# One place later: the large products beside scores and context sums in an attention kernel

## The reference, cut to what matters

```python
h_q = (x @ w_q.T).reshape(b, lq, H, DH)          # x normalised
h_k = (key_value_states @ w_k.T).reshape(b, lk, H, DH)
h_v = (key_value_states @ w_v.T).reshape(b, lk, H, DH)
score = jnp.einsum('bqhd,bkhd->bhqk', h_q, h_k) + position_bias[None]
score = jax.nn.softmax(jnp.where(m, score, -jnp.inf), axis=-1)
attn = jnp.einsum('bhqk,bkhd->bqhd', score, h_v).reshape(b, lq, H * DH)
out = attn @ w_out.T                             # then the residual, and the feed-forward layer
```

## Time and profile before

| | us |
|---|---|
| median of three runs | 820.9 (820.55 to 822.34) |
| the profiled execution | 820.63, its span 818.8 |
| TensorE busy | 799.6 (98% of the span) |
| VectorE busy | 636.1 (78%) |
| ScalarE busy | 361.6 (44%) |
| GpSimd busy | 305.9 (37%) |
| TensorE's granted clock, mean | 0.999 |
| attention rounds 3 to 13 | about 409 to 731 |

### The profile page before, as it was taken

How to read it: one execution, slowest core, us unless ns; L and a number is a source line. 1 busy time by engine, 2 the same in 40 slices (tenths; PEclk the granted TensorE clock), 3 DMA queues, 4 the chain that set the end, 5 groups by cost and what they waited for, 6 DMA issues and landing times.

```text
span 818.8 us, 12698 instructions
## 1 busy us (share of the span) xinstructions
PE 799.6 (98%) x4090; PEld 674.9 (82%) x4090; DVE 636.1 (78%) x1066; ACT 361.6 (44%) x949; POOL 305.9 (37%) x279
## 2 busy tenths in 40 slices
PE   9999999999999999999999999999999999999998
PEld 8888888888888888887888887888788888888886
DVE  6877868977873796988878877877877787777775
ACT  6633432432331344544444444444444444447683
POOL 3103111021020034726455545635545544545136
PEclk9999999999999999999999999999999999999999
DMA  8365575584474749337556565565655646653002
GB/s 305 131 219 175 191 245 168 156 289 133 155 228 158 242 163 313 127 101 229 158 177 211 159 205 187 156 198 178 209 167 172 227 149 207 187 186 142 1 1 104
DMA packets 103217, 145.54 MB, mean 178 GB/s; under 512 B 9944, under 2 KB 74584, under 8 KB 97648
## 3 DMA queue, kind: packets, MB, share of 16 engines
q1 hardware_dynamic: 102720, 144.33, 54.5%
q10 hardware_dynamic: 432, 0.39, 0.1%
HBM read 93.31 MB, written 51.38 MB: 177 GB/s over the span
## 4 chain that ended last, share of the span: by engine, by line
PE 95%; issue 2%; DVE 1%; ACT 1%; DMA 0%; POOL 0%; SPq 0%; DVEq 0%
PE out L1438 11%; PE out L1440 11%; PE out L1439 11%; PE proj L1438 10%; PE proj L1440 10%; PE proj L1439 10%; PE o L1558 7%; PE s L1532 7%; PE s L1439 4%; PE s L1440 4%; PE s L1438 4%; PE proj L1634 1%; PE proj L1635 1%; PE t L1586 1%; PE t L1542 1%
## 5 line engine op out<-in xcount | busy, mean ns | idle before, releaser
L1005 ACT ACTIVATE probs<-probs,neg_max 128x128 f32<-128x128 f32 x256 | 99.7, 391 | 120.6 <-DVE neg_max L1270 120.6
L835 POOL TENSOR_TENSOR w_stage<-w_stage 128x256 f32<-128x256 f32 x30 | 26.7, 892 | 278.2 <-DMA w_stage<-in_wk 242.1
L1438 PE MATMUL out<-wo_hi,o_hi 128*128 128x512 f32 x224 | 91.6, 409 | 13.2 <-issue 13.2
L847 POOL TENSOR_TENSOR w_lo<-w_stage,w_hi 128x512 fp32r<-128x512 f32 (+1 forms) x52 | 64.3, 1245 | 101.3 <-ACT w_hi L951 101.3
L1440 PE MATMUL out<-wo_lo,o_hi 128*128 128x512 f32 x224 | 88.0, 393 | 0.0
L1439 PE MATMUL out<-wo_hi,o_lo 128*128 128x512 f32 x224 | 87.4, 390 | 0.0
L1438 PE MATMUL proj<-x_hi,w_hi 128*128 128x512 f32 x210 | 85.3, 406 | 0.9 <-POOL w_lo L847 0.6
L1315 DVE TENSOR_TENSOR acc<-out,acc 128x512 f32<-128x512 f32 x100 | 67.8, 678 | 20.5 <-PE out L1440 20.5
L1440 PE MATMUL proj<-x_lo,w_hi 128*128 128x512 f32 x210 | 82.4, 392 | 0.0
L1439 PE MATMUL proj<-x_hi,w_lo 128*128 128x512 f32 x210 | 82.0, 391 | 0.0
L859 POOL TENSOR_TENSOR bias_mask<-bias_raw,mask_neg 128x512 f32<-128x512 f32 x64 | 76.2, 1191 | 13.0 <-DVE probs L1267 11.8
(11 more groups left out here) (360 smaller groups left out, 2078.4 us busy)
## 6 DMA issues: line engine op xcount, KB each, us to landing
k_spill<-ring SPq DMA_DIRECT2D x64, 256.0 KB, 3.5
v_spill<-ring SPq DMA_DIRECT2D x64, 256.0 KB, 2.6
p_turned<-probs SPq DMA_DIRECT2D x208, 64.0 KB, 1.8
probs_t<-p_turned SPq DMA_DIRECT2D x52, 256.0 KB, 4.0
big_stage<-in_wv SPq DMA_DIRECT2D x8, 1024.0 KB, 7.5
w_stage<-in_wq SPq DMA_DIRECT2D x32, 256.0 KB, 3.1
k_first<-k_spill SPq DMA_DIRECT2D x8, 1024.0 KB, 6.0
v_first<-v_spill SPq DMA_DIRECT2D x8, 1024.0 KB, 5.0
```

The lines of the kernel that those rows point to most:

```text
L847: pool.tensor_tensor(lo, staged(m, part), hi.bitcast(F32), ALU.subtract).then_inc(g_wlo, 1)
L1005: last = act.activation(probs[:, j % 2, b, :], probs[:, j % 2, b, :], ACT.Exp, bias=neg_max[:, col:col + 1], accum_out=row_sum[:, col:col ...
L1438: pe.matmul(to[:], left_hi, right_hi, start=first and n == 0, stop=False, skip_group_check=True)
```

## The change

The number of steps is the same, each on the same engine; only the order of the list is different, in the rounds 0 to 13. In rounds 2 to 13, for TensorE:

| place | large products before | after |
|---|---|---|
| A | OUT0, P1, OUT1, OUT2 | P4 of the group before, OUT0, P1, OUT1 |
| B | OUT3, P6, OUT4, P2 | OUT2, OUT3, P6, OUT4 |
| C | OUT5, OUT6, P5, OUT7 | P2, OUT5, OUT6, P5 |
| D | P7, P3, P4 | OUT7, P7, P3 |

With OUT7 the split of the next output weights ("WO") moves from the end of C into D. The loads of query weights move from the middle of C to the end of B, their four sums ("WS") from the end of D to its early steps. Round 0 ends with one output product fewer, and round 1 takes it over. In round 13 P4 stays where it is, and "WO" moves as in the others.

```diff
--- before.py
+++ after.py
@@ -275,23 +275,24 @@
             steps += [("S", 3), *product(first, 4), *prod[2], ("WX", m, 3), ("T", 2), ("EXP", 3), ("BM", 4), *prod[5], ("N", 3),
                       ("PV", 2), ("WOL", 1), *load]
             steps += [*prod[7], ("S", 4), *prod[3], ("T", 3), ("EXP", 4), ("BM", 5), ("BL", 4), *prod[4],
-                      *outs(0, 0), *normal(4), ("KL", 2), *sums, *outs(0, 1, 2)]
+                      *outs(0, 0), *normal(4), ("KL", 2), *sums, *outs(0, 1)]
             continue
         o = p - 1
         final = 2 * p + 2 == SPLIT
+
         if p == 1:
-            steps += aside(j, outs(o, 3) + prod[1], [*outs(o, 4), ("WX", m, 1)], [])
-            steps += aside(j + 1, outs(o, 5) + prod[6], [("VV", p + 1), ("WX", m, 2), ("WX", m, 3)], prod[2])
-            steps += aside(j + 2, outs(o, 6) + prod[5], [*outs(o, 7), ("WO", p), *load], [])
+            steps += aside(j, outs(o, 2, 3), [*prod[1], ("WX", m, 1)], outs(o, 4))
+            steps += aside(j + 1, prod[6], [("VV", p + 1), *outs(o, 5), ("WX", m, 2), ("WX", m, 3)], prod[2] + load)
+            steps += aside(j + 2, outs(o, 6), prod[5], [])
         else:
-            steps += aside(j, outs(o, 0) + prod[1], [*outs(o, 1), ("WX", m, 1)], outs(o, 2))
-            steps += aside(j + 1, outs(o, 3) + prod[6], [("VV", p + 1), *outs(o, 4), ("WX", m, 2), ("WX", m, 3)], prod[2])
-            steps += aside(j + 2, outs(o, 5, 6), [*prod[5], *load], [*outs(o, 7), ("WO", p)])
+            steps += aside(j, product(n - 1, 4) + outs(o, 0), [*prod[1], ("WX", m, 1)], outs(o, 1))
+            steps += aside(j + 1, outs(o, 2, 3), [*prod[6], ("VV", p + 1), ("WX", m, 2), ("WX", m, 3)], outs(o, 4) + load)
+            steps += aside(j + 2, prod[2] + outs(o, 5), outs(o, 6), prod[5])
         if final:
-            steps += aside(j + 3, prod[7] + prod[3], [("WOL", p + 1), ("PV", j + 2), *prod[4], ("KL", p + 2), *sums, ("WO", p + 1)],
+            steps += aside(j + 3, outs(o, 7) + [("WO", p)] + prod[7], [*prod[3], ("WOL", p + 1), ("PV", j + 2), *prod[4], ("KL", p + 2), ("WO", p + 1)],
                            [*outs(p, 0, 1), ("PV", j + 3), ("VV", p + 2)])
         else:
-            steps += aside(j + 3, prod[7] + prod[3], [("WOL", p + 1), *prod[4], ("KL", p + 2), *sums], [])
+            steps += aside(j + 3, sums[:1] + outs(o, 7) + [("WO", p)] + prod[7], [*prod[3], ("WOL", p + 1), ("KL", p + 2), *sums[1:]], [])
```

## The result

The changed kernel takes 842.11 us (median of 4 runs, 841.92 to 843.19), the kernel before 821.21 us beside it (4 runs, 820.55 to 822.34): ratio 1.0256, 95% interval 1.0238 to 1.0273. The prediction was 806.3, so its sign is wrong. Lines of the changed kernel have numbers one higher than before (L1285 is now L1286).

What follows compares the result with a forecast made beforehand. TensorE, busy 98% of the span, was taken as the bound, so only its waits could be regained. 15.7 gained less 1.1, Step 5 at zero: 14.6 off 820.63 gives 806.0, against the median 806.3; range 803 to 812.

Steps and rivals of the forecast that it cites:

- Step 3: OUT7 and WO to the front of D: wo_lo ready at +8.85, OUT0 free 0.13 before its turn; cost 0.
- Step 1: P4 ahead of OUT0 in A: OUT0 free at +2.63, turn at +3.16; stall goes, 1.43 x 11 = 15.7 us.
- Step 2: P1 in A needs VectorE's C21: free at +4.55, turn at +4.53; 0 to 0.44 us a round, taken as 0.1.
- Step 4: Query weight loads at the end of B, sums in D from +1.3 to near +4.3, clear of the normalisation: no cost.
- Step 5: Rounds 1 and 2 and the exit from the last round: sum 0, bounds -2 (gain) to +2 us.
- Wait moves: OUT0 or P1 waits about 1 us a round, for late weights or VectorE's backlog: 816.2 us; chance 0.16.
- The slower rival: End of D: wo_lo overtakes the normalisation, which waits until +8.85; 3.0 us a round, 838 us; chance 0.06.

Runs made afterwards that it cites:

- Experiment 9: Changed kernel, but OUT7 of the pairs up to 12 multiplies parts of x_hi and x_lo, and the copy o_hi no longer waits for it: 808.65 us.
- experiment 6: Changed kernel with OUT7 and the split WO one block later in D, behind P7 instead of ahead of it: 865.31 us.
- experiment 8: Changed kernel with OUT7 back at the end of C and P5 in its turn in D, the split WO staying in D: 808.7 us, ratio 0.9847.
- experiment 4: Kernel before with P4 alone moved, from the end of D to the head of A in rounds 2 to 13: 822.45 us.
- experiment 5: Kernel of experiment 8 with the loads of query weights back in C and their sums back at the end of D: 839.32 us.
- experiment 3: Kernel before with only OUT7 and the split WO moved, from the end of C to the head of D in rounds 2 to 13: 871.35 us.
- experiment 10: Kernel of experiment 8 with P5 of round 1 left in C of that round: 808.46 us, ratio 0.984.
- experiment 7: Kernel of experiment 1 with the four pair sums put ahead of wo_lo on GpSimd: 833.46 us.
- experiment 1: Changed kernel with OUT7 and the split WO back at the end of C, P5 taking OUT7's turn in D: 818.62 us, ratio 0.9967.

## Why the prediction was wrong, by its own steps

**Step 3 failed, and alone turned the sign.** It said: "In D ScalarE first has the exponentials. In C they end at +5.42". The time was taken over from C, where nothing holds the copy. What the step didn't ask: who else waits for OUT7? It knew OUT7 as a reader of the weights ("wo_hi may be overwritten only after OUT7"). But OUT7 also *reads* o_hi, and that buffer is written again by the first copy in D. The exponentials end at +7.76 (441.24) instead of +5.42, wo_lo is 2.33 late, and OUT0 waits 1.90. Experiment 9 takes that one dependence away and gives 808.65; experiment 6 lengthens it by a block, and it grows by a block.

**Step 1 was right**, with one condition that it didn't state. Its turn and its o_lo were met within 0.02 in experiment 8, and the rounds lasted 27.91 against its 27.84 plus 0.1. But P4 alone gives nothing (experiment 4): there D is a block shorter, and o_lo is late all the same.

**Step 2 was right**: P1 is released by C21 in nearly every round, 0.74 behind its start, and at about the cost taken: in experiment 8 the places A of rounds 4 to 13 last 7.35 to 7.45, where 7.30 is unstalled.

**Step 4 was right that early sums cost nothing and leave the normalisation's time** (first sum +1.47 of D, 434.95; predicted +1.3), and too modest: it named this as an aside, and experiment 5 shows that, with the split in D, the whole gain hangs on it; experiment 4 points the same way. A run of the kernel before with the loads and sums alone moved is missing. Its sentence "uncovered it would cost one for one through wo_lo" was right in kind: in experiment 3 wo_lo is late, the sums stand behind it, and 21.3 of the 50 us that the run is slower are P1's waits for w_lo.

**Step 5** (rounds 1, 2 and the exit at 0, from -2 to +2): experiment 8's profiled execution took 808.35 against 820.63. The eleven rounds give back 11 x (29.27 - 27.91) = 15.0, so that 820.63 - 15.0 = 805.6 and 2.7 us were lost outside them, 0.7 beyond the bound. Putting P5 of round 1 back (experiment 10) returns none of it. The largest part, 1.5 us, lies behind round 13. There a place lasts 6.54 us, where the kernel before has 5.07, and TensorE waits 0.75 for the normalisation. The timeline of experiment 8 has:

```profile
727.47 2.38 POOL L890 TENSOR_TENSOR x_lo<-scales_raw,x_lo 8x1024 fp32r<-8x1024 f32 x1
...
728.18 1.69 DVE L1277 TENSOR_TENSOR inv_sum<-inv_sum,row_valid 128x4 f32<-128x4 f32 x1
```

VectorE's small instruction ends with GpSimd's again (729.87 and 729.85). In the kernel before it comes as GpSimd's is nearly done, and takes 0.16. Place A of round 3, at 7.98, is another 0.6 longer than those that follow it.

**The rivals.** "Wait moves" named the right victim (OUT0 waiting for wo_lo) at 1 us a round beside a lost stall of 1.43; OUT0 waits 1.90 to 1.96, and place A is 2.43 longer than unstalled. Its price was taken from margins, not from a cause. The slower rival, wo_lo overtaking the normalisation, lies near the time measured (838 against 842.1), but its mechanism isn't what happened: L1286 at 441.68 is before wo_lo at 442.26 and takes its 0.70. Both were late together. That the rival is real, experiment 7 shows: 833.46. The chance of 0.06 for slower was too low because o_hi's readers were left out of the working.

**The rule weighed in the prediction.** In experiment 7, L1277 ended with the GpSimd instruction that began before it; in experiment 1 both parts of the normalisation were stretched by the pair sums. The Trainium skill, "SBUF — State Buffer", section "SBUF: two separate sides", says that VectorE with two SBUF inputs and GpSimd exclude each other on one port pair for the whole instruction; these traces agree.

## What to carry to other kernels

When an instruction is moved later, list not only who waits for what it writes, but who overwrites what it reads: with single buffers that next writer may be the first instruction of a chain, and the whole chain moves. A table of waits with a strange releaser (a copy that waits for a product that it doesn't use) is the sign of it. And times of one place may be taken over for another only after the first instruction's waits were checked there; parts of a change may also need each other: here P4 alone gave nothing and OUT7 alone a loss.

## What the runs showed of the hardware that was not expected

**The granted clock falls after some waits and not after others.** The changed kernel, at the head of A of round 4 (columns as above):

```profile
443.00:444.00 1.00, 0.00 (x0) 0.00 (x0) 1.00 (x3) 0.00 (x0) 1.00 (x1) 1.00 0.01 2
...
446.00:447.00 1.00, 1.00 (x4) 0.78 (x3) 0.22 (x1) 1.00 (x7) 0.43 (x1) 0.50 0.77 205
```

After 1.90 us without a matmul the clock stood at 0.50 (1.2 of 2.4 GHz) for some 3.4 us, with matmuls 0.43 apart instead of 0.23. It did so in four of eleven rounds (4, 7, 10 and 13, every third), for 1.35 us each, 5.4 of the 21.4 us; in the other seven, after a wait just as long (1.90 to 1.96 in all eleven), it stayed at 1.00. What tells them apart stays open. So the price of a wait of 2 us can be 2 or 3.3 us.

**A VectorE instruction of 0.16 us can cost 1.43** when GpSimd starts first, and 1.69 in experiment 8. In experiment 7 GpSimd's next instruction also started ahead of VectorE's next one (443.14 before 443.25), so that VectorE, with a short instruction ahead of a long one, lost twice.
